# Moving the list tables of the first expert slots, on VectorE, from the scan of the last block to its opening

## What is computed

```python
# first layer: state space model with a gate
xn = layernorm(x)
s  = sigmoid(silu(xn @ s_w1.T + s_b1) @ s_w2.T + s_b2)
u  = (xn @ B_w.T + B_b) * s
h[t] = h[t-1] @ A.T + u[t]                       # recurrence over 4096 tokens
y  = h @ C_w.T + C_b + xn @ D_w.T + D_b
x1 = x + y * sigmoid(xn @ g_w.T + g_b)
# second layer: one of 8 experts for each token
xn1 = layernorm(x1)
e   = argmax(xn1 @ gate_w.T)
out = x1 + xn1 + xn1 @ expert_w[e].T
```

## Time and profile before

| what | value |
|---|---|
| median of the runs before | 911.41 us (909.81 to 911.87) |
| the profiled execution's own time | 910.55 us |
| its span, first to last instruction | 908.8 us |
| granted TensorE clock, mean | 0.996 |
| PE busy | 890.0 us (98%) |
| DVE busy | 685.2 us (75%) |
| ACT busy | 635.7 us (70%) |
| POOL busy | 428.5 us (47%) |

### The profile page before, as it was taken

How to read it: one execution, slowest core, us unless ns; L and a number is a source line. 1 busy time by engine, 2 the same in 40 slices (tenths; PEclk the granted TensorE clock), 3 DMA queues, 4 the chain that set the end, 5 groups by cost and what they waited for, 6 DMA issues and landing times.

```text
span 908.8 us, 15716 instructions
## 1 busy us (share of the span) xinstructions
PE 890.0 (98%) x4413; PEld 719.9 (79%) x4414; DVE 685.2 (75%) x1697; ACT 635.7 (70%) x880; POOL 428.5 (47%) x671
## 2 busy tenths in 40 slices
PE   8999999999999999999999999999999999999996
PEld 7777878787887878787787878787878887888884
DVE  6777888888888878888787878888787465555552
ACT  5568687978878787978778787978534446666661
POOL 1134546282836546282826446282614454433442
PEclk9999999999999999999999999999999999999998
DMA  8436395858668495857778495856989979998871
GB/s 316 134 93 149 86 218 129 204 141 198 148 169 196 106 221 123 195 148 199 153 170 188 113 214 121 201 146 160 288 284 400 389 232 266 219 221 220 196 184 49
DMA packets 231051, 172.37 MB, mean 190 GB/s; under 512 B 155702, under 2 KB 189238, under 8 KB 229953
## 3 DMA queue, kind: packets, MB, share of 16 engines
q1 hardware_dynamic: 220032, 137.71, 61.3%
q0 software_dynamic: 10800, 33.70, 11.0%
q10 hardware_dynamic: 144, 0.07, 0.0%
HBM read 81.63 MB, written 54.68 MB: 150 GB/s over the span
## 4 chain that ended last, share of the span: by engine, by line
PE 84%; DVE 7%; issue 2%; DMA 1%; SPq 1%; ACT 1%; POOLq 0%; DVEq 0%; ACTq 0%
PE y L1774 19%; PE gates L1476 6%; PE y L1476 6%; PE y L1478 6%; PE y L1477 6%; PE gates L1477 6%; PE gates L1478 6%; PE turned L1661 3%; PE gates L1661 3%; PE scan L1620 3%; PE scan L1476 2%; PE scan L1478 2%; PE scan L1477 2%; PE turned L1763 2%; PE gates L1665 1%
## 5 line engine op out<-in xcount | busy, mean ns | idle before, releaser
L1774 PE MATMUL y<-experts,x1T_hi 128*128 x568 | 180.5, 399 | 0.0
L666 POOL DMA_INDIRECT out<-gate,ids x71 | 73.0, 1028 | 107.3 <-DVE gate L1441 67.2
L602 POOL TENSOR_SCALAR ln_var_eps<-ln_mean_var 128x4 f32<-128x4 f32 x16 | 3.7, 232 | 253.2 <-DVE ln_mean_var L1097 253.2
L1774 PEld LDWEIGHTS y<-experts,x1T_hi 128*128 128x128 f32 x568 | 103.2, 188 | 19.9 <-issue 0.2
L1774 PE MATMUL y<-experts,x1T_lo 128*128 x284 | 111.4, 392 | 0.0
L1476 PE MATMUL gates<-GwT_hi,xT_hi 128*128 128x512 f32 x256 | 104.7, 409 | 1.4
L592 POOL TENSOR_TENSOR y_biased<-y_biased,gate 128x256 f32<-128x256 f32 x120 | 94.0, 806 | 23.9 <-DVE y_biased L1087 23.9
L1476 PE MATMUL y<-DwT_hi,xT_hi 128*128 128x512 f32 x256 | 102.6, 401 | 0.5 <-DVE gateT L1019 0.5
L1441 DVE TENSOR_TENSOR gate<-y,raw_weights 128x512 f32<-128x512 f32 x71 | 49.1, 691 | 68.6 <-PE y L1774 42.6
L1477 PE MATMUL gates<-GwT_lo,xT_hi 128*128 128x512 f32 x256 | 100.6, 393 | 0.0
L1478 PE MATMUL gates<-GwT_hi,xT_lo 128*128 128x512 f32 x256 | 100.6, 393 | 0.0
(11 more groups left out here) (285 smaller groups left out, 2337.5 us busy)
## 6 DMA issues: line engine op xcount, KB each, us to landing
raw_weights<-routed_rows SPq DMA_DIRECT2D x71, 258.0 KB
x_in<-L_attn_x SPq DMA_DIRECT2D x32, 512.0 KB, 4.2
x_rows<-L_attn_x SPq DMA_DIRECT2D x32, 512.0 KB, 4.7
turned_experts<-raw_weights SPq DMA_DIRECT2D x32, 512.0 KB, 3.5
experts<-turned_experts SPq DMA_DIRECT2D x8, 2048.0 KB
raw_weights<-L_ffn_expert_w SPq DMA_DIRECT2D x32, 256.0 KB, 3.1
routed_rows<-padrow SPq DMA_DIRECT2D x9, 258.0 KB
out<-gate,ids POOLq DMA_INDIRECT x71
```

The source lines that it names most:

```text
L666: nc.gpsimd.indirect_dma_start(out=out_rows, out_offset=bass.IndirectOffsetOnAxis(ap=ids[r][:, 0:1], axis=0), in_=res[r], in_offset=None, ...
L1774: ins = nc.tensor.matmul(Y[m % 2][:], x2T[a][:, k, m % 2 * P:(m % 2 + 1) * P], flat[:, bass.ds(first + (w * KD + k) * D, D)], start=(k == ...
```

## The change

VectorE does `list_tiles` and `list_gaps` ahead of the first `silu_product` of the last block, `slot_experts` between the first `silu_product` and the first `silu_lo`, and `slot_rows` behind the two statistics and ahead of `low_piece`. The three old places are empty. A wait for `run_ready` at `LASTB - 1` stands ahead of the first table instruction. The operations themselves, and every other engine's list, are as before.

```diff
@@ -1267,12 +1267,18 @@
                 if ahead and tail:
                     ln1_stats(b + 1, 0)
                     ln1_stats(b + 1, 1)
+                elif not ahead:
+                    dve.wait_ge(S_["run_ready"], LASTB - 1)
+                    list_tiles(0)
+                    list_gaps()
                 for m in range(KH):
                     silu_product(b, m)
                     if not tail:
                         prep(2 + m)
                     elif ahead:
                         ln1_stats(b + 1, 2 + m)
+                    elif m == 0:
+                        slot_experts(0, FIRST)
                     silu_lo(b, m)
@@ -1285,6 +1291,8 @@
                     powers_lo()
                 elif ahead:
                     ln1_mv(b + 1)
+                else:
+                    slot_rows(0, FIRST)
@@ -1311,8 +1319,6 @@
                 over(b, 1)
                 gate_sum(b, 0)
-                if not ahead:
-                    list_tiles(0)
                 over(b, 2)
@@ -1326,16 +1332,11 @@
                 if tail and ahead and not dma:
                     low_piece(b, 0)
-                if not ahead:
-                    list_gaps()
-                    slot_experts(0, FIRST)
                 over(b, 5)
                 if dma:
                     tail_lo(old, 3)
                 elif ahead:
                     low(b + 1, 0)
-                else:
-                    slot_rows(0, FIRST)
                 to_middles(b)
```

## The result

The change makes the kernel slower by some 0.3%: median 914.55 us (913.46 to 915.41, 8 runs) against 911.68 (909.81 to 912.65, 8 runs), ratio 1.0025 [1.0014, 1.0036]. Repeated later it gave 914.48 against 911.58, ratio 1.0032 [1.0020, 1.0043]. That is +2.9 us both times, at the upper end of the prediction's range (914.2, which is +2.8 over the 911.41 that it counts from; in microseconds 914.55 lies 0.35 above it). It is not the forecast's own case but the time of the slower rival (+2.1 to +3.1).

What follows compares the result with a forecast made beforehand. TensorE was taken to bound the kernel, with the slots following it at a fixed pace. Opening +1.9 us less scan 1.5 us made +0.4 us, forecast 911.8 us on the median's scale, range 909.8 to 914.2.

Steps and rivals of the forecast that it cites:

- the forecast's own case: Opening of last block: two held instructions pass per GpSimd boundary, cost near the gain, +0.4 us, 911.8 us; chance 0.48.
- the slower rival: Ahead of the first `silu_product` one instruction passes per GpSimd boundary: net +2.1 to +3.1 us, 913.5 to 914.5; chance 0.30.
- What bounds the kernel, and the scan: TensorE sets the pace; at the scan's end it waits for VectorE and the tables, 1.5 us together.
- the predicted gain of 1.5 us: End of the scan: removing the tables from VectorE ends both TensorE pauses, gaining 1.5 us.
- These instructions are held beside GpSimd.: Opening: fourteen of 16 table instructions wait for GpSimd; with only the eight two-input ones held, the kernel gains about 1.1 us.
- passes at once (0.55): Opening, behind the first `silu_product`: `slot_past` isn't held beside GpSimd and takes 0.55 us.
- Two held instructions (0.19 us apart) pass at each boundary.: Opening: nine table instructions need five GpSimd instruction ends, so `silu_product` starts at 640.5 instead of 638.60.
- the sum's +0.4: Whole kernel: opening cost of 1.9 us less scan gain of 1.5 us, so +0.4 us.
- The rest of the opening: From second `silu_lo` to first scan step: `silu_lo` at 645.6 against 645.16 wanted; `u_in_pairs` and scan step 1.9 us late.
- The opening costs nothing: Opening without GpSimd contention: VectorE's idle time, 1.19 us ahead of `silu_product` and 2.04 ahead of `u_in_pairs`, covers the tables.
- The rows' load: First slot: SyncE's load moves up to 2.8 us earlier, counted as nothing; without that, 0.6 us would be given back.
- Whatever the last block gains or loses comes out at the end one for one.: Slots: they follow TensorE at a fixed pace, passing on its whole gain or loss while their inputs keep up.

Runs made afterwards that it cites:

- the two variants in pieces: Kernel before, scan's tables cut into smaller pieces within the scan: first 911.75 us, ratio 1.0000; second, four instructions one step earlier still, 912.15 us, ratio 0.9997.
- the nine moved ahead: Kernel after, with the nine instructions of `list_tiles` and `list_gaps` ahead of `y_biased` instead of behind it: 912.98 us, ratio 1.0011.

## Why the prediction was only partly right

*What bounds the kernel, and the scan.* Right. Both pauses went; the predicted gain of 1.5 us measured 1.42 in the first profile after (from +3.33 at the first scan step to +1.91 at `down`) and 5.33 − 3.81 = 1.52 in the second.

*"These instructions are held beside GpSimd."* Right, and for the single-input ones too, which the forecast had taken from one CAST: the conversion and shift on 8 elements took 0.59 to 0.67. `slot_past` was not free in the first profile after, as the prediction had it ("passes at once (0.55)"), but took 1.07; in the second it took 0.54. The sum was free, as predicted.

*"Two held instructions (0.19 us apart) pass at each boundary."* This is the step that failed. The table instructions stand 0.03 us apart where they are held (638.42 to 638.45), and even that is enough for GpSimd's next instruction to take hold. Only one passes; a second one does where GpSimd pauses for 0.08 us between its multiplications and its additions, which is one boundary in four (the prediction had GpSimd run "without a break"). The CAST at 452.67 that had suggested two was a single passage, read as a rule: the subtraction right behind it was held (0.58 us instead of 0.29).

```profile
452.94 0.58 DVE L1044 TENSOR_TENSOR chunk_ends<-z,chunk_ends 128x124 fp32r<-128x124 f32 x1
```

Nine instructions took 4.6 us in one execution and 5.7 in two, not the predicted 3.1, and the first `silu_product` was 3.4 to 5.0 late, not 1.9. The Trainium skill (SBUF — State Buffer, section "SBUF: two separate sides") states the stricter reading: whichever of the two engines starts first keeps the shared pair for its whole instruction, and the other blocks fully. The rows of the nine agree with it. The CAST doesn't quite: it passed at 452.67, though the profile lets GpSimd's second instruction begin at 452.53. Read so, the rule made the slower rival the likelier one, and it had been given 0.30 against 0.48. That rival was itself priced too high in one place (6 us from `y_biased` to `silu_product`, measured 4.6 and 5.7, since the pauses let a second one through). That the time still came out near the range's upper end is that rival's doing and not the sum's +0.4.

*The rest of the opening.* The product with `s_w2` was 2.6 and 3.6 us late instead of 0.45, and that carried most of the loss. `u_in_pairs` then started 3.13 us behind that product in both profiles after, where it was 2.28 before: 0.85 more, with `slot_rows` filling the idle time (648.18 to 649.65, 1.47); it was priced with 0.3 of hold and had none. In sum the first scan step came 3.33 and 5.33 us late against 1.9 predicted, where the slower rival had 3.6 to 4.6.

*Slack.* "The opening costs nothing" where it isn't contested counted the 1.19 us ahead of `silu_product` as free. They were also the cover for a late copy of the input, seen in three of twelve profiles (0.33, 0.33, 0.68 us of wait). And behind the pause of TensorE that the hold makes the clock can fall (once in the three profiles with such a pause of over 2 us in the opening ahead of the product with `s_w2`), which was in no term of the sum.

*The rows' load.* The prediction said that SyncE's load would move up by as much as 2.8 us, and that SyncE wasn't held by anything else. It was: the wait at L485 is now ended by the landing of `turned_experts`, 2.1 us. ScalarE got the rows 40.75 us into the block instead of 37.95, later by 2.8 while TensorE's turn came 2.0 later, so the slack of 0.92 was used up: TensorE started on them 0.45 us behind its last product (675.57 to 676.02) where it was 0.23 before, some 0.2 us lost. In the second profile after it was 0.23 again. The table, ready some 19 us earlier, was of no use to anyone.

*"Whatever the last block gains or loses comes out at the end one for one."* Only roughly, since a transfer stands in between. In ten of the twelve profiles TensorE goes on at slot 7 to 8 1.42 or 1.43 us behind the VectorE `gate` that waits for the first slots' store. From GpSimd's issue of that store to this `gate` it took 11.5 and 11.7 us before (50.62 to 62.14 and 62.37 in the block), 11.9 and 13.6 in the two variants in pieces, 12.1 and 11.0 after, and 13.0 to 13.6 with GpSimd held back, with the nine moved ahead and with GpSimd's instructions halved. So the landing does move with its issue, and adds some 2.5 us of scatter of its own. Of the seven edits that left slot 0 between 0.86 earlier and 0.66 later than before, six took 0.4 to 3.6 us more at slot 7 to 8 and one 0.2 less; with slot 0 2.42 late it took 4.58. With one profile each, it is open whether an edit or chance makes the store slow. So the +2.9 us of the medians is made of the opening (+3.3 to +5.3), the scan (−1.4 to −1.5) and the slots (+1.5 or −0.3 by execution), less up to 0.6 us by which the two profiles of the kernel before differ. Of the first profile's +1.5 behind slot 0, 0.33 stand at slot 7 to 8 and 1.07 at slot 24 to 25, and the second profile has neither.

## What to carry to other kernels

A small VectorE instruction on SBUF beside a busy GpSimd costs the rest of GpSimd's current instruction, however small it is (the reductions here, and those with an input in PSUM, were not held): price a chain of n such instructions at n GpSimd instructions (here six to eight of nine, at 0.62 to 0.70 us for 0.16 us of work each), and put such chains where GpSimd is silent, or make GpSimd's instructions shorter. Idle time ahead of an instruction is only free if it doesn't already absorb something that varies from execution to execution, so look at the same spot in several profiles. Before a gain ahead of a long stage is counted, look for a transfer in that stage whose own time scatters by more than the gain.

## What the runs showed of the hardware that was not expected

- The hold is not shortened by how little the VectorE instruction has to read: 8 elements on one partition waited 0.59 to 0.67 us beside GpSimd instructions of 0.72, and 0.38 beside those of 0.43. A gap of 0.03 us between two VectorE instructions (638.42 to 638.45) was too long to pass together.
- TensorE's clock fell to its lower level behind a pause of 3.41 us, and in another run behind one of only 2.00 us (granted clock 0.50 from 702 to 704), but not behind pauses of 2.44, 2.41, 2.07 and 2.03 us. So the length of the pause alone doesn't tell. Behind the first of them matmuls of 512 columns stood 0.42 us apart until 653.26. Of the six executions of the kernel after in that comparison four had a mean granted clock of 0.993 or 0.994; all 13 of the kernel before had 0.997 or 0.998.
- Delaying GpSimd by 3 us moved the hold to other instructions rather than away: CAST and subtraction of the scan's first split went from 0.30 and 0.43 to 0.79 and 0.90 us.
